# Scan inputs for four states at a time on four 32-row tiles of TensorE

## The chip, the cores and the metric

The kernel runs on one core of one Trainium2 chip. The metric is device microseconds of one launch, the median of several runs. In this text PE is TensorE, DVE is VectorE, ACT is ScalarE, POOL is GpSimd, SP is SyncE (it issues the DMAs).

## The reference, cut to what matters

A four-layer state-space model (Mamba blocks) runs over 16 sequences of 64 context tokens and then 512 tokens, width 256, inner width 512, 16 states; after it comes a cross-attention block with an MLP. All is fp32. What the change touches is the scan input of each layer:

```python
xi = silu(conv(...)); dt = softplus(...)            # [B, S, 512]
dA  = exp(dt[..., None] * A)                        # [B, S, 512, 16]
dBu = dt[..., None] * Bm[:, :, None, :] * xi[..., None]
h = da * h + dbu                                    # a step of the scan over time
y = einsum('bes,bs->be', h, c)                      # sum over the 16 states
```

## The kernel before

**Steps.** Time is always 512 positions. A step is one layer for 512 positions: 8 steps come first for the contexts (two halves, four layers; "the context steps"), then four blocks of 16 steps (four sequences, four layers; "the main steps"), each block followed by the attention. The 512 inner channels are 4 groups (`c`) of 128 partitions, so a step has 4 x 16 = 64 scans of 128 x 512, one for each state and group. They go in 32 units `v` of two states, 8 units to a group.

**One unit.** ACT writes the two decays `dA` (L673, three units ahead, ring of 8). PE writes the two inputs `dBu` into PSUM: `make_input` (L437) multiplies `dtxT` (time on partitions, `dt * xi`) by `diagB`, a diagonal matrix of -B that POOL builds (L1147). Before, the 128 rows of time are two tiles of 64 rows; each tile writes its own bank, and the columns hold (time, state) with two states side by side. Each unit has two banks of four, so the inputs of unit v+1 are made while unit v is scanned: PE waits only for the scans up to unit v-1 (L432). DVE runs the two scans (L912) and reads the PSUM columns at a stride of two. POOL multiplies both by C (L1139). PE sums the states with transposes into one accumulator (`sum_pair`, L454, for unit v-2); ACT takes it out when a group ends (L684).

**The other work of a step** (norm, projections, convolution taps, softplus, gate, residual) belongs to the step before or to the ones after, and is placed by hand in tables: `MAIN_PE`, `MAIN_ACT`, `MAIN_DVE`, `MAIN_POOL` say behind which unit each piece stands on its engine, with the number of steps that it is ahead; `PRE_*` say it for the context steps. A DVE event could stand behind either scan of a unit. PE's pieces share three PSUM banks (`MAIN_BANK`). Each engine goes through its list in order; semaphores tie them. PE pieces: `xi`, `z`, `out` (projections, L479, L484, L517), `xp` (L490), `dt` (L500), `dxT` (L505), `yt` (L510), `bT` (L494), `ms` (L473). DVE events: `tap` (L940), `q` (L946), `less` (L951), `ndt` (L957), `gate` (L962), `res` (L967), `norm` (L922). POOL: `dtx` (L1159), whose result `dxT` turns. SP issues the loads of C, of initial states and of weights (`body` of the last block below).

Of the kernel before, what the change touches and what calls it, by code (L numbers as in the profile page):

```python
# [38 lines left out]
PRE_BANK = {"yt3": 0, "out0": 0, "out1": 1, "dxT1": 0, "dt3": 1, "dxT2": 2, "dxT3": 2, "ms": 0, "xi0": 0, "xi1": 1,  # L39
            "xi2": 2, "xi3": 0, "yt0": 1, "z0": 2, "z1": 0, "z2": 2, "xp": 1, "z3": 0, "bT": 1, "yt1": 0, "dt0": 2,  # L40
            "dt1": 1, "yt2": 0, "dxT0": 0, "dt2": 2}
MAIN_BANK = {"xi0": 0, "xi1": 2, "xi2": 1, "xi3": 0, "dt3": 2, "yt3": 1, "out0": 1, "xp": 2, "dxT3": 0, "bT": 0,
             "dt0": 2, "out1": 1, "yt0": 0, "z0": 0, "dxT0": 2, "z1": 1, "dt1": 2, "yt1": 0, "z2": 1, "z3": 0,
             "dt2": 2, "dxT1": 1, "ms": 0, "yt2": 1, "dxT2": 2}
# [1329 lines left out]
```

## Time and profile before

| what | value |
|---|---|
| median of 3 runs | 9753.2 us (9751.4 to 9761.05) |
| the profiled execution | 9749.7 us, span 9747.6 us |
| PE busy | 8898.7 us, 91% |
| DVE busy | 7469.1 us, 77% |
| POOL busy | 6517.7 us, 67% |
| ACT busy | 5984.7 us, 61% |
| mean granted clock of PE | 0.962 |

Busy time is the union of the instructions of an engine. The mean duration of an instruction is longer than its share of the busy time where several are in flight at once. A matmul in fp32 is two PE instructions, a transpose is one.

### The profile page before, as it was taken

Reading aid. Unit: us, or ns where it says so; the run is one execution under the profiler, and the core shown is the slowest. Engines: PE = TensorE matmul, PEld = TensorE weight load, DVE = VectorE, ACT = ScalarE, POOL = GpSimd, SP = SyncE. Lnnn points to the kernel's source line nnn. Section 1 sums busy time; section 2 is a strip of 40 time slices with the busy share of each in tenths; the row PEclk is TensorE's granted clock in tenths of the full one; section 3 lists DMA queues with packets and bytes.
Section 4 is the critical chain, followed back from the end, with each engine's and each line's share of the span. In section 5 each row is a group of like instructions: output and inputs, shape, how many; then the busy total and the mean of one; then the engine's idle time right before and its main releaser. Section 6 shows DMA issues by size and latency. Waiting matters only on the chain.

```text
span 9747.6 us, 188863 instructions
## 1 busy us (share of the span) xinstructions
PE 8898.7 (91%) x67488; PEld 6199.9 (64%) x67488; DVE 7469.1 (77%) x7810; ACT 5984.7 (61%) x9252; POOL 6517.7 (67%) x3556
## 2 busy tenths in 40 slices
PE   8999799999998799999988799999988799999988
PEld 5666466666664566666654576666654576666654
DVE  5778688888873588888873688888873688888872
ACT  6666576666743566676642566667642666766642
POOL 5878577788761477787751477887751577877750
PEclk9999899999999899999999899999999899999999
DMA  1111111111100111111100111111100111111100
GB/s 56 46 46 41 54 42 39 42 43 55 39 33 6 56 42 39 42 49 48 39 32 7 55 42 39 46 52 42 39 32 8 54 42 39 54 46 40 39 32 9
DMA packets 132793, 390.13 MB, mean 40 GB/s; under 512 B 49520, under 2 KB 77620, under 8 KB 94984
## 3 DMA queue, kind: packets, MB, share of 16 engines
q1 hardware_dynamic: 131848, 377.75, 11.0%
q8 instruction: 566, 9.27, 0.4%
q14 instruction: 379, 3.10, 0.1%
HBM read 364.46 MB, written 13.24 MB: 39 GB/s over the span
## 4 chain that ended last, share of the span: by engine, by line
POOL 48%; issue 38%; PE 3%; POOLq 1%; DVE 1%; ACT 0%; DVEq 0%; ACTq 0%
POOL arena L1139 40%; POOL arena L1147 5%; POOL arena L1159 2%; PE ps L540 1%; POOL arena L1177 1%; PE ps L621 1%; POOLq L1135 1%; DVE arena L1080 0%; DVE arena L1071 0%; ACT arena L824 0%; PE ps L587 0%; PE ps L616 0%; PE ps L517 0%; POOLq L314 0%; DVE arena L1084 0%
## 5 line engine op out<-in xcount | busy, mean ns | idle before, releaser
L1139 POOL TENSOR_TENSOR arena<-arena 128x1024 f32<-128x1024 f32 x2304 | 5441.6, 2366 | 1471.4 <-DVE arena L912 1428.0
L912 DVE TENSOR_TENSOR_SCAN arena<-arena,ps 128x512 f32<-128x512 f32 x4608 | 5606.8, 1259 | 763.1 <-PE ps L437 589.7
L673 ACT ACTIVATE arena<-arena,rate 128x512 f32<-128x512 f32 (+1 forms) x4608 | 3103.8, 713 | 782.7 <-DVE arena L912 771.0
L437 PE MATMUL ps<-arena 64*128 64x128 f32 x36864 | 2711.3, 287 | 345.7 <-DVE arena L912 343.0
L437 PEld LDWEIGHTS ps<-arena 64*128 64x128 f32 x36864 | 2266.8, 189 | 775.4 <-DVE arena L912 481.1
L454 PEld LDWEIGHTS ps<-csts,arena 128*128 128x128 f32 x18432 | 2133.2, 143 | 839.5 <-issue 622.5
L454 PE MATMUL ps<-csts,arena 128*128 128x128 f32 x18432 | 2462.4, 277 | 32.9 <-POOL arena L1139 32.9
L1159 POOL TENSOR_TENSOR arena<-arena 128x512 f32<-128x512 f32 x288 | 365.5, 1269 | 778.5 <-DVE arena L957 778.5
L1147 POOL TENSOR_TENSOR arena<-csts,arena 128x512 f32<-128x512 f32 x576 | 608.5, 1059 | 76.3 <-ACT arena L764 76.3
L788 ACT ACTIVATE arena<-arena,Dall 128x512 f32<-128x512 f32 x288 | 208.3, 723 | 719.3 <-POOL arena L1159 719.3
L517 PE MATMUL ps<-arena 128*128 128x512 f32 x1152 | 630.5, 641 | 7.6 <-DVE arena L962 4.4
L484 PE MATMUL ps<-arena 128*128 128x512 f32 x1152 | 634.7, 642 | 2.7 <-DVE arena L940 2.7
L479 PE MATMUL ps<-arena 128*128 128x512 f32 x1152 | 577.6, 628 | 34.0 <-DVE arena L922 33.4
L540 PE MATMUL ps<-arena 128*128 128x512 f32 (+2 forms) x1152 | 564.4, 646 | 31.7 <-ACT arena L884 16.2
L1177 POOL TENSOR_TENSOR arena<-arena 128x512 f32<-128x512 f32 x128 | 133.2, 1042 | 601.4 <-DVE arena L1074 601.4
L684 ACT ACTIVATE arena<-ps 128x512 f32<-128x512 f32 x288 | 170.8, 593 | 592.5 <-PE ps L454 591.8
L940 DVE SCALAR_TENSOR_TENSOR ps<-arena,ps 128x512 f32<-128x512 f32 x576 | 427.3, 742 | 90.4 <-ACT ps L727 86.8
L540 PEld LDWEIGHTS ps<-arena 128*128 128x128 f32 (+1 forms) x1152 | 240.7, 218 | 372.2 <-issue 350.0
L1106 DVE COPY arena<-ps 128x256 f32<-128x256 f32 x64 | 27.2, 425 | 478.2 <-PE ps L621 478.2
L824 ACT ACTIVATE arena<-ps 128x512 f32<-128x512 f32 (+1 forms) x252 | 137.5, 585 | 387.9 <-PE ps L540 319.5
L951 DVE SCALAR_TENSOR_TENSOR ps<-arena,ps 128x512 f32<-128x512 f32 x288 | 198.0, 687 | 193.5 <-ACT ps L779 192.8
L479 PEld LDWEIGHTS ps<-arena 128*128 128x128 f32 x1152 | 202.9, 195 | 224.7 <-issue 178.3
(102 smaller groups left out, 7640.7 us busy)
## 6 DMA issues: line engine op xcount, KB each, us to landing
arena<-c_rows SPq DMA_DIRECT2D x288, 1024.0 KB, 4.7
arena<-ip_x SPq DMA_DIRECT2D x20, 512.0 KB, 3.6
arena<-ip_z SPq DMA_DIRECT2D x20, 512.0 KB, 3.6
arena<-op_w SPq DMA_DIRECT2D x20, 512.0 KB, 3.9
hT<-xT SPq DMA_DIRECT2D x16, 512.0 KB, 5.2
arena<-w SPq DMA_DIRECT2D x8, 1024.0 KB
out<-arena SPq DMA_DIRECT2D x64, 128.0 KB, 1.7
arena<-xp_w SPq DMA_DIRECT2D x20, 160.0 KB, 2.5
```

Of the source, the lines that this page charges most:

```text
L437: i = nc.tensor.matmul(o, dtxT[rows, c, b, :], diagB[rows, pair, b, :].rearrange("p (i s) -> p i s", s=2), start=True, stop=True)
L454: i = nc.tensor.matmul(acc[:, b * P:(b + 1) * P], hs[:, place(n, v) + s, b * P:(b + 1) * P], eye, start=False, stop=(v + 1) % CU == 0 and ...
L479: i = nc.tensor.matmul(o, ipx[:, k, c * P:(c + 1) * P], xn[:, k, :], start=k == 0, stop=k == KD - 1)
L484: i = nc.tensor.matmul(o, ipz[:, k, c * P:(c + 1) * P], xn[:, k, :], start=k == 0, stop=k == KD - 1)
L517: i = nc.tensor.matmul(o, opw[:, k, c * P:(c + 1) * P], zs[:, par, k, :], start=k == 0, stop=k == KI - 1)
L540: last = nc.tensor.matmul(o, lhs, rhs, start=i == 0, stop=i == len(parts) - 1)
L673: nc.scalar.activation(o, i, ACT.Exp, scale=rate[:, ph.layer(n), g:g + 1]).then_inc(decay.sem, 1)
L912: nc.vector.tensor_tensor_scan(hs[:, place(n, v) + g % 2, :], dA[:, g % RING, :], both[:, g % 2::2], init[:, n % 2, g:g + 1] if ph.main() ...
L940: i = nc.vector.scalar_tensor_tensor(o, w, taps[:, c, k:k + 1], acc_c, ALU.mult, ALU.add)
L1139: nc.gpsimd.tensor_tensor(hs[:, a:a + 2, :], hs[:, a:a + 2, :], Crep[:, 2 * pair:2 * pair + 2, :], ALU.mult).then_inc(prod.sem, 1)
L1147: nc.gpsimd.tensor_tensor(diagB[:, pair, :, :].rearrange("p b (i s) -> p b i s", s=2), minus64.unsqueeze(1).unsqueeze(3).broadcast_to([P, ...
L1159: nc.gpsimd.tensor_tensor(dtx, dt[:, c, :], xs[:, m % 2, c, :], ALU.mult).then_inc(dtx_ready.sem, 1)
```

## The change

Scans are served in sets of four states ("quads"): a set fills all four banks. There are 16 sets in a step instead of 32 pairs. The time rows of `dtxT` are now four tiles of 32 rows, each with a bank of its own, 16 matmuls (32 PE instructions) to a set; the scans read at a stride of four. Set w may be written only when the last scan of set w-1 is done, and it stands at the end of an odd unit on PE, behind that unit's pieces and sum. DVE events now stand only behind both scans of a unit, and the tables place all of them behind odd units, so between the sets. `diagB` is built in four instructions instead of eight a step, `zs` (the z branch) has three buffers instead of two and the z projections are made a step ahead. All tables and bank assignments are new; pieces `xp`, `out`, `xi`, `z`, `ms` are cut less finely. In the context steps one SILU table load and one LOG_EXP load go.

```diff
+Q = 4
+QUADS = G // Q
+CQ = DS // Q
+ZS = 3
...
+MAIN_PE = {2: [("xi3", 1), ("z0", 1)], 4: [("dt3", 0), ("z1", 1)], 6: [("yt3", -1), ("z2", 1)],
+           8: [("xp.0", 1), ("xp.1", 1), ("z3", 1)], 9: [("xp.2", 1), ("xp.3", 1)], 10: [("out0.0", -1), ("out0.1", -1)],
+           11: [("out0.2", -1), ("out0.3", -1)], 12: [("bT", 1), ("dt0", 1)], 13: [("dxT3", 0)],
+           14: [("yt0", 0), ("out1.0", -1)], 15: [("out1.1", -1), ("out1.2", -1)], 16: [("out1.3", -1), ("dt1", 1)],
+           18: [("ms", 2)], 20: [("dxT0", 1)], 22: [("yt1", 0)], 23: [("dt2", 1)], 24: [("dxT1", 1)], 25: [("xi0", 2)],
+           28: [("yt2", 0), ("xi1", 2)], 30: [("dxT2", 1)], 31: [("xi2", 2)]}
+MAIN_DVE = {1: [("tap12", 1), ("tap20", 1)], 3: [("tap21", 1), ("tap22", 1)], 5: [("tap30", 1), ("tap31", 1), ("tap32", 1)],
+            7: [("q3", 0), ("gate3", -1)], 9: [("less3", 0)], 11: [("ndt3", 0)], 13: [("res0", -1)],
+            15: [("q0", 1), ("gate0", 0)], 17: [("less0", 1), ("res1", -1), ("ndt0", 1)], 19: [("q1", 1)],
+            21: [("less1", 1), ("norm0", 2), ("ndt1", 1)], 23: [("norm1", 2), ("gate1", 0)], 25: [("q2", 1)],
+            27: [("less2", 1), ("tap00", 2), ("ndt2", 1)], 29: [("gate2", 0), ("tap01", 2), ("tap02", 2)],
+            31: [("tap10", 2), ("tap11", 2)]}
+MAIN_POOL = {12: [("dtx3", 0)], 18: [("dtx0", 1)], 22: [("dtx1", 1)], 28: [("dtx2", 1)]}
+PRE_PE = {0: [("dxT1", 0)], 2: [("dxT2", 0)], 3: [("yt3", -1)], 4: [("dxT3", 0), ("out0", -1)], 5: [("out1", -1)],
+          8: [("ms", 1)], 12: [("xi0", 1), ("xi1", 1)], 13: [("xi2", 1)], 15: [("xi3", 1)], 16: [("yt0", 0)],
+          18: [("z0", 1), ("z1", 1)], 20: [("z2", 1), ("z3", 1)], 21: [("xp", 1)], 22: [("yt1", 0)], ...
...
-                pe.wait_ge(state.sem, state.at(ph, n, 2 * v - 2))
+                pe.wait_ge(state.sem, state.at(ph, n, Q * w))
                 for b in range(NB):
-                    for h in range(2):
-                        rows = slice(64 * h, 64 * h + 64)
-                        o = input_ps[:, bank + h, :].rearrange("p (i b s) -> p i b s", b=NB, s=2)[:, :, b, :]
+                    for r in range(4):
+                        rows = slice(32 * r, 32 * r + 32)
+                        o = input_ps[:, r, :].rearrange("p (i b s) -> p i b s", b=NB, s=Q)[:, :, b, :]
...
             def body(ph, n):
                 for v in range(UNITS):
-                    to, w = ahead(ph, n, v + 1)
-                    if to is not None:
-                        make_input(ph, to, w)
                     for m, name in events(ph.pe_at, ph, n, v):
                         job(ph, m, name)
                     to, w = ahead(ph, n, v - 2)
                     if to is not None and (scans(ph, n) or n == ph.steps):
                         sum_pair(ph, to, w)
+                    to, w = ahead(ph, n, v + 1)
+                    if to is not None and v % 2:
+                        make_input(ph, to, w // 2)
...
+                if g % Q == 0:
+                    dve.wait_ge(input_ready.sem, input_ready.at(ph, n, g // Q + 1))
...
-                nc.vector.tensor_tensor_scan(hs[:, place(n, v) + g % 2, :], dA[:, g % RING, :], both[:, g % 2::2],
+                nc.vector.tensor_tensor_scan(hs[:, place(n, v) + g % 2, :], dA[:, g % RING, :], quad[:, g % Q::Q],
```

## Rows read from the trace of the kernel before

**Rows 1.** The page: busy time by engine, and the chain that ended last.
```profile
PE 8898.7 (91%) x67488; PEld 6199.9 (64%) x67488; DVE 7469.1 (77%) x7810; ACT 5984.7 (61%) x9252; POOL 6517.7 (67%) x3556
...
POOL 48%; issue 38%; PE 3%; POOLq 1%; DVE 1%; ACT 0%; DVEq 0%; ACTq 0%
```

**Rows 2.** Busy time in two single main steps and six context steps (columns named above them).
```profile
core 0: us, PE busy (x) PEld busy (x) DVE busy (x) ACT busy (x) POOL busy (x), PEclk, DMA share, GB/s
1208.10:1319.00 110.90, 105.24 (x889) 76.47 (x888) 96.93 (x98) 77.09 (x119) 88.04 (x46) 1.00 0.11 42
1319.00:1429.90 110.90, 106.70 (x889) 77.81 (x888) 96.93 (x97) 77.17 (x119) 88.05 (x45) 0.98 0.15 50
...
199.50:907.90 708.40, 658.05 (x5325) 480.44 (x5324) 558.44 (x577) 476.69 (x726) 565.72 (x457) 0.95 0.14 46
```

**Rows 3.** Groups by line, ten main steps (1208.1 to 2316.7 us).
```profile
L912 DVE TENSOR_TENSOR_SCAN arena<-arena,ps 128x512 f32<-128x512 f32 x640 | 784.0, 1266 | 102.2 <-PE ps L437 92.2 <-ACT arena L673 10.1
...
L437 PE MATMUL ps<-arena 64*128 64x128 f32 x5120 | 375.1, 286 | 48.1 <-DVE arena L912 48.0
...
L1139 POOL TENSOR_TENSOR arena<-arena 128x1024 f32<-128x1024 f32 x321 | 758.5, 2367 | 228.7 <-DVE arena L912 227.5
L1147 POOL TENSOR_TENSOR arena<-csts,arena 128x512 f32<-128x512 f32 x80 | 84.8, 1060 | 0.0
L1159 POOL TENSOR_TENSOR arena<-arena 128x512 f32<-128x512 f32 x40 | 50.8, 1270 | 0.0
```

**Rows 4.** Timeline, PE and DVE, where the scans wait for PE.
```profile
2017.09 2.45 DVE L912 TENSOR_TENSOR_SCAN arena<-arena,ps 128x512 f32<-128x512 f32 x2
...
2018.66 1.04 PE L454 MATMUL ps<-csts,arena 128*128 128x128 f32 x8
...
2019.62 1.16 PE L437 MATMUL ps<-arena 64*128 64x128 f32 x16
...
2020.71 1.12 PE L517 MATMUL ps<-arena 128*128 128x512 f32 x2
2020.92 2.45 DVE L912 TENSOR_TENSOR_SCAN arena<-arena,ps 128x512 f32<-128x512 f32 x2 [1.39 <-PE ps L437]
...
2021.68 0.64 PE L505 MATMUL ps<-csts,arena 128*128 128x128 f32 x4
```

**Rows 5.** Timeline where taps stand between scans.
```profile
1985.34 1.16 PE L437 MATMUL ps<-arena 64*128 64x128 f32 x16
...
1986.43 1.98 PE L479 MATMUL ps<-arena 128*128 128x512 f32 x4
...
1988.99 0.73 DVE L940 SCALAR_TENSOR_TENSOR ps<-arena,ps 128x512 f32<-128x512 f32 x1
...
1989.76 0.75 DVE L940 SCALAR_TENSOR_TENSOR arena<-arena,ps 128x512 f32<-128x512 f32 x1
...
1990.42 1.28 DVE L912 TENSOR_TENSOR_SCAN arena<-arena,ps 128x512 f32<-128x512 f32 x1
```

**Rows 6.** Timeline of the four column tiles in the attention: the burst, its first 0.03 us.
```profile
2957.77 1.94 PE L587 MATMUL ps<-arena 128*32 128x512 f32 x8 [5.30 <-ACT arena L824]
...
2957.77 1.08 PE L587 MATMUL ps<-arena 128*32 128x512 f32 x4 [5.30 <-ACT arena L824]
```

**Rows 7.** Busy time and granted clock in short stretches, columns as in rows 2.
```profile
1332.70:1336.10 3.40, 1.41 (x15) 1.17 (x14) 3.36 (x5) 2.38 (x5) 0.85 (x2) 1.00 0.04 3
...
1336.10:1339.50 3.40, 3.40 (x24) 2.94 (x22) 3.40 (x5) 3.37 (x3) 2.23 (x2) 0.50 0.46 154
...
1443.50:1446.90 3.40, 1.41 (x14) 1.17 (x12) 3.36 (x5) 2.38 (x5) 0.85 (x2) 1.00 0.00 0
1446.90:1450.30 3.40, 2.09 (x24) 1.73 (x24) 3.40 (x5) 3.37 (x3) 2.31 (x1) 1.00 0.00 0
```

**Rows 8.** Timeline of PE where the clock is at 0.50.
```profile
1335.88 1.90 PE L437 MATMUL ps<-arena 64*128 64x128 f32 x16 [1.99 <-DVE arena L912]
1337.70 1.96 PE L454 MATMUL ps<-csts,arena 128*128 128x128 f32 x8
```

More of the change, by code:

```diff
@@ L36 @@
 SILU = "silu_and_others"
[L39 to L44, printed above, removed]
@@ L72 @@
-MAIN_PE = {0: [("xi2", 1)], 1: [("xi3", 1)], 2: [("dt3", 0)], 3: [("yt3", -1)], 5: [("out0.0", -1)],
[7 rows of a table removed]
-MAIN_ACT_FIRST = {2: [("yev3", -1)], 10: [("yev0", 0)], 18: [("yev1", 0)], 26: [("yev2", 0)]}
-MAIN_ACT = {0: [("xi1", 1)], 1: [("xi2", 1)], 2: [("xi3", 1)], 3: [("dt3", 0)], 4: [("silu_z", 0), ("silu_x", 1)],
[4 rows of a table removed]
-MAIN_DVE = {(0, 0): [("tap02", 1)], (0, 1): [("tap10", 1)], (1, 0): [("tap11", 1), ("tap12", 1)],
[6 rows of a table removed]
-MAIN_POOL = {7: [("dtx3", 0)], 15: [("dtx0", 1)], 23: [("dtx1", 1)], 28: [("dtx2", 1)]}
+PRE_BANK = {"dt0": 2, "dt1": 0, "dt2": 2, "dt3": 0, "dxT0": 1, "dxT1": 1, "dxT2": 2, "yt3": 1, "out0": 0, "out1": 2,
+            "dxT3": 1, "ms": 1, "xi0": 0, "xi1": 2, "xi2": 1, "xi3": 0, "yt0": 2, "z0": 2, "z1": 1, "z2": 2, "z3": 0,
+            "xp": 1, "yt1": 0, "bT": 1, "yt2": 1}
@@ new lines @@
+MAIN_BANK = {"xi0": 2, "xi1": 1, "xi2": 2, "xi3": 0, "z0": 1, "z1": 1, "z2": 1, "z3": 1, "dt3": 2, "yt3": 0, "xp": 0,
+             "out0": 1, "bT": 0, "dt0": 2, "dxT3": 0, "yt0": 0, "out1": 1, "dt1": 0, "ms": 2, "dxT0": 1, "yt1": 1,
+             "dt2": 0, "dxT1": 1, "yt2": 0, "dxT2": 0}
+PARTS = {"ms": KD, "xi": KD, "z": KD, "xp": KI, "out": KI}
+PRE_PE = {0: [("dxT1", 0)], 2: [("dxT2", 0)], 3: [("yt3", -1)], 4: [("dxT3", 0), ("out0", -1)], 5: [("out1", -1)],
[4 rows of a table added]
+PRE_ACT_FIRST = {2: [("yev3", -1)], 10: [("yev0", 0)], 18: [("yev1", 0)], 26: [("yev2", 0)]}
@@ new lines @@
+PRE_ACT = {0: [("ln3", 0)], 1: [("dxT1", 0), ("skip2", 0)], 3: [("dxT2", 0), ("skip3", 0)], 5: [("dxT3", 0)],
[4 rows of a table added]
+PRE_DVE = {1: [("less3", 0), ("ndt3", 0)], 3: [("gate3", -1)], 5: [("res0", -1)], 7: [("res1", -1)],
[6 rows of a table added]
+PRE_POOL = {0: [("dtx2", 0)], 2: [("dtx3", 0)], 28: [("dtx0", 1)], 30: [("dtx1", 1)]}
+MAIN_PE = {2: [("xi3", 1), ("z0", 1)], 4: [("dt3", 0), ("z1", 1)], 6: [("yt3", -1), ("z2", 1)],
[5 rows of a table added]
+MAIN_ACT_FIRST = {2: [("yev3", -1)], 10: [("yev0", 0)], 18: [("yev1", 0)], 26: [("yev2", 0)]}
+MAIN_ACT = {0: [("xi2", 1)], 3: [("xi3", 1), ("z0", 1)], 5: [("dt3", 0), ("z1", 1)], 6: [("silu_z", 0), ("silu_x", 1)],
[4 rows of a table added]
@@ L198, in program @@
         Crep = view(DS, T)
-        diagB = view(CU, NB, 128)
+        diagB = view(CQ, NB, P)
         dA = view(RING, T)
@@ L204, in program @@
         xs = view(2, KI, T)
-        zs = view(2, KI, T)
+        zs = view(ZS, KI, T)
         xbc = view(2, NB, DS)
@@ L516, in job @@
                     for k in parts:
-                        i = nc.tensor.matmul(o, opw[:, k, c * P:(c + 1) * P], zs[:, par, k, :],
+                        i = nc.tensor.matmul(o, opw[:, k, c * P:(c + 1) * P], zs[:, m % ZS, k, :],
                                              start=k == 0, stop=k == KI - 1)
@@ L729, in event @@
                 elif name[0] == "z":
-                    if m > 1:
-                        await_done(act, ph, m - 2, "out1")
+                    if m >= ZS:
+                        await_done(act, ph, m - ZS, "out1")
                     await_done(act, ph, m, name)
-                    nc.scalar.activation(zs[:, par, c, :], job_bank(ph, name), ACT.Copy).then_inc(read_of(ph, name), 1)
+                    nc.scalar.activation(zs[:, m % ZS, c, :], job_bank(ph, name), ACT.Copy).then_inc(read_of(ph, name), 1)
                 elif name == "silu_z":
-                    nc.scalar.preload_act_table_set(SILU)
-                    await_read_of(act, ph, m, "z2")
-                    await_read_of(act, ph, m, "z3")
-                    nc.scalar.activation(zs[:, par, :, :], zs[:, par, :, :], ACT.Silu).then_inc(silu.sem, 1)
+                    if ph.main():
+                        nc.scalar.preload_act_table_set(SILU)
+                    for k in (3,) if ph.main() else (1, 2, 3):
+                        await_read_of(act, ph, m, f"z{k}")
+                    nc.scalar.activation(zs[:, m % ZS, :, :], zs[:, m % ZS, :, :], ACT.Silu).then_inc(silu.sem, 1)
                     if not ph.main() or m + 1 == ph.steps:
@@ L747, in event @@
                     nc.scalar.activation(xs[:, par, :, :], xs[:, par, :, :], ACT.Silu).then_inc(silu.sem, 1)
-                    nc.scalar.preload_act_table_set(LOG_EXP)
+                    if ph.main():
+                        nc.scalar.preload_act_table_set(LOG_EXP)
                 elif name == "xp":
@@ L961, in event @@
                     await_done(dve, ph, m, f"yt{c}")
-                    nc.vector.tensor_tensor(zs[:, par, c, :], job_bank(ph, f"yt{c}"), zs[:, par, c, :], ALU.mult
+                    nc.vector.tensor_tensor(zs[:, m % ZS, c, :], job_bank(ph, f"yt{c}"), zs[:, m % ZS, c, :], ALU.mult
                                             ).then_inc(read_of(ph, f"yt{c}"), 1)
@@ L974, in body @@
                             scan(ph, n, 2 * v + s)
-                        for m, name in events(ph.dve_at, ph, n, (v, s)):
-                            event(ph, m, name)
+                    for m, name in events(ph.dve_at, ph, n, v):
+                        event(ph, m, name)
             def begin(ph):
@@ L1140, in product, with diag @@
                                         ).then_inc(prod.sem, 1)
-            def diag(ph, m, pair):
-                if pair == 0:
+            def diag(ph, m, quad):
+                if quad == 0:
                     await_read_of(pool, ph, m, "bT")
-                pool.wait_ge(input_ready.sem, input_ready.at(ph, m - 1, UNITS - CU + pair + 1))
-                nc.gpsimd.tensor_tensor(diagB[:, pair, :, :].rearrange("p b (i s) -> p b i s", s=2),
-                                        minus64.unsqueeze(1).unsqueeze(3).broadcast_to([P, NB, 64, 2]),
-                                        xbc[:, m % 2, :, 2 * pair:2 * pair + 2].unsqueeze(2).broadcast_to([P, NB, 64, 2]),
+                pool.wait_ge(input_ready.sem, input_ready.at(ph, m - 1, QUADS - CQ + quad + 1))
+                shape = [P, NB, 32, Q]
+                nc.gpsimd.tensor_tensor(diagB[:, quad, :, :].rearrange("p b (i s) -> p b i s", s=Q),
+                                        minus32.unsqueeze(1).unsqueeze(3).broadcast_to(shape),
+                                        xbc[:, m % 2, :, Q * quad:Q * quad + Q].unsqueeze(2).broadcast_to(shape),
                                         ALU.mult).then_inc(diag_ready.sem, 1)
@@ L1168, in body @@
                         event(ph, m, name)
-                    if v >= UNITS - CU and ph.has(n, 1):
-                        diag(ph, n + 1, v - (UNITS - CU))
+                    if v >= UNITS - CU and v % 2 == 0 and ph.has(n, 1):
+                        diag(ph, n + 1, (v - (UNITS - CU)) // 2)
             def attend(ph):
@@ L1314, in _inputs @@
     p = np.arange(P)
-    cst = np.zeros((P, 321), np.float32)
+    cst = np.zeros((P, 289), np.float32)
     cst[:, 0:128] = p[:, None] == p[None, :]
     cst[:, 128:256] = 1.0 / D
-    cst[:, 256:320] = -1.0 * (p[:, None] % 64 == p[None, :64])
-    cst[DR + DS, 320] = 1.0
+    cst[:, 256:288] = -1.0 * (p[:, None] % 32 == p[None, :32])
+    cst[DR + DS, 288] = 1.0
     cst_attention = np.zeros((P, 424), np.float32)
```

30 lines of the change are left out of this document (12 added, 18 removed), and 51 rows, old and new, of tables (MAIN_ACT, MAIN_DVE, MAIN_PE, PRE_ACT).

## The prediction, made before the changed kernel ran

> **What bounds the kernel now.** I read the page's busy line and chain first. PE is busy for 91% of the span, DVE 77%, and the chain gives POOL 48% and issue 38% [rows 1]. That chain is a poor guide: POOL's products sit idle 227.5 us in ten main steps waiting for scans [rows 3], so POOL follows. Then I cut the span into steps. A main step takes 110.9 us; in it PE is busy 105.2 to 106.7, DVE 96.9, POOL 88.0, ACT 77.1 [rows 2]. There are 64 such steps, so 64 x 110.9 = 7095 us of the 9749.7 of the profiled execution; the 8 context steps are 118.1 each (708.4 / 6, rows 2), 945 us; the rest, some 1710 us, is attention and the ends of the blocks, which the change leaves alone. Third, who waits: the scans wait 92.2 us in ten steps for the inputs (L437), 9.2 a step, and the inputs wait for scans 48.0 [rows 3]. The timeline shows how: transposes, inputs and a projection follow each other on PE without a hole while the scans stand idle 1.39 us [rows 4]. So PE bounds long parts of a step, DVE is 14 us below it.
>
> **What goes.** A pair of inputs holds PE for 2020.71 - 2019.62 = 1.09 us [rows 4], 32 times a step, 34.9 us (the union is 37.5, rows 3). Its 16 instructions last 1.16 us together, and 8 single transposes of the same 128 columns last 1.04 [rows 4], so in the pair two instructions run at a time. A set has 32 instructions. If four run at a time, a set costs what a pair does now: 16 x 1.1 = 17.5 us a step, 17.4 less than before. Four row tiles are in no row. The nearest is the attention's four column tiles: eight instructions in 1.94 us, of which four start within 0.03 us and last to 1.08 [rows 6], so four at a time there. The bounds are 1.1 us a set (four at a time) and 2.0 (two at a time, as the 64-row tiles now); I take 1.1, the value by the column tiles. Four `diagB` instructions of 1.06 [rows 3] go from POOL, 4.2 us a step, as good as nothing, since POOL waits for the scans; so do two table loads in a context step, as ACT has 34 us of slack in a step [rows 2].
>
> The Trainium skill (TensorE: Matmul & The Clock Gate, Part 3 on packing) gives 3.07 times for four row tiles of K=32 at N=512. No run here shows it; by it a set would be near 1.1 us as well, and two at a time unlikely.
>
> **What comes: a wait at each set.** Before, inputs for the next pair were made under a scan. Now PE may start a set only when the fourth scan ends. From the end of a scan to the first input: scans end at 2017.09 + 2.45 = 2019.54, the inputs start at 2019.62, 0.08. From there to the next scan: 2020.92 - 2019.62 = 1.30 [rows 4]. Scans follow each other every 2.45 - 1.27 = 1.18 us [rows 3, 4]. So from the fourth scan's start to the fifth's: 1.27 + 0.08 + 1.30 = 2.65 instead of 1.18, and a set takes 3 x 1.18 + 2.65 = 6.19 us. Sixteen are 99.0 us, with room of 1.47 us for vector work at each boundary. The 32 events of a step cost (96.9 - 78.4) / 32 = 0.58 each [rows 2, 3], dependent taps 0.77 and 0.66 [rows 5]. One or two of them fit; five boundaries have three: behind v=5 three taps (2.2, so 0.7 over), behind 17, 21, 27 and 29 about 1.75 (0.3 over each), together 1.8. DVE's own path is then 100.8 us. A boundary with one event (9, 11, 13, 19, 25) leaves some 0.9 us of DVE empty. The stride of four on the PSUM reads has no row; scans at a stride of two take 1.18; I take 0 and hold 0 to 0.03 us for it, 2 us a step at most.
>
> **Where PE is late for a boundary.** Of 6.19 us the set takes 1.09 and two sums 2 x 0.96 [rows 4], which leaves 3.2 for pieces. Four 512-column instructions take about 1.83 (1.98 with the tail, rows 5), two 0.97, four transposes about 0.5 [rows 4], the start of a group 0.44 more (in sets 1, 5, 9, 13). By the new table, in sets (units 2w, 2w+1):
> - set 1: `xi3` and `z0`, 3.66 + 0.44: 0.9 late;
> - set 4: `xp` 3.66 and `z3` 1.83: 2.3 late;
> - set 5: `out0` 3.66 + 0.44: 0.9 late;
> - set 7: `yt0`, three parts of `out1`, 3.3: 0.1 late;
> - set 6: the pieces fit, but PE waits for POOL. `dtx3` stands behind product 12: 1.18 + 1.27 until unit 12 is scanned, 2.37 for its product, 1.27 for `dtx3` [rows 3], 6.09 us after the set's first scan. Then `dxT3` 0.5, sum 11 0.96, and 1.30: the next scan starts at 8.85, 2.7 late. Before, the same pieces stood two units apart.
> All others need 2.9 or less. Together 6.9, so 107.7 us a main step if PE runs at its full clock, 3.2 less than 110.9. The context steps have the same boundaries; there set 2 (`dxT3`, `out0`, `out1`) and set 10 (`z2`, `z3`, `xp`) are each over 4 us late, set 6 (three `xi`) 2.3, set 9 0.9, and 4 or 5 us of events lie over: 99 + 11.7 + 5 = 115.6, 2.5 less. ACT must make 64 decays and needs 77.1 us in all, POOL 84: neither gets to the path but through `dtx3`. The SP queue issues the same DMAs; `ipz` is loaded later in relation to its first use (20 units ahead still) and `init`, `cinit` and C's rows keep their place, so nothing there. Sum so far: 64 x -3.2 + 8 x -2.5 = -225 us.
>
> **The clock.** The granted clock of PE is at one of two levels, 2.4 GHz (1.00) and 1.2 (0.50). Between 1332.7 and 1336.1 PE was busy 1.41 of 3.4 us, having waited 1.99 us for a scan; in the next 3.4 us the clock was 0.50, though PE was busy throughout. The same stretch one step later, 1443.5, brought no fall [rows 7]. In the main steps this is the one hole, and the fall comes in every second step (1.00 and 0.98, rows 2). At the low clock the inputs last 1.90 instead of 1.16 and eight transposes 1.96 instead of 1.04 [rows 8]. The change makes many such holes: in sets 0, 10 and 13 PE has 0 to 0.5 us of pieces, so it stands 2.7 to 3.2 us of 6.19 idle; sets 6 (the wait for `dtx3`) and 11 have 1.6 to 2.5. A hole of 2 us now brings a fall in half of the cases; so I take 3 falls a step. A fall of 3.4 us takes 1.7 us of PE's work; behind set 0 it lies on set 1, which is late already and pays all of it; elsewhere the boundary pays 0.8 to 0.9 for the slow set, and the sums and pieces doubled use up the slack. The floor is 0 (falls only in slack, as now), the ceiling five falls of 1.7, 8.5 us. I take 3 x 1.7 = 5.0 a step, in a context step 4 (it falls already to 0.95, rows 2): +320 + 32 = +352 us.
>
> The Trainium skill (TensorE: Matmul & The Clock Gate, "HAM oscillation") tells of kernels whose gaps in matmul work bring the low clock back over and over. It speaks against this change; rows 7 show the fall behind such a gap, with the 3.4 us.
>
> **Sum.** 9749.7 - 225 + 352 = 9877; the profiled execution is 3.5 below the median, so 9880 us, 1.3% slower.
>
> **Rivals.**
> - *The clock stays up where it counts.* All steps as above, but the falls hit slack: 0 to 1 us a step. For it: now a fall every second step costs nothing that shows, 110.9 with and without [rows 2]. Against: those steps wait for something else there, and a set at the low clock now is on DVE's path. 9753 - 225 + 40 = 9570 us, faster. It decides from 3.5 us of falls a step: under that the change wins.
> - *Two tiles at a time.* The change doesn't do what it says: 32-row tiles start in twos. Each set is 0.9 longer; 11 boundaries pay all, 5 about 0.6, and PE saves nothing: 13 us a step, so 107.7 + 13 + some 4 of falls = 124.5; 9753 + 64 x 13.6 + 8 x 10 = 10700 us. For it: two at a time is all that row tiles show [rows 4]. Against: rows 6.
> - *The terms cancel*, 3.5 us of falls against 3.2 of gain: 9750, no change.
>
> **How the numbers follow.** Forecast 0.50 (its own range 9770 to 10010: falls of 4 to 7 us), the clock rival 0.30, two at a time 0.13, cancelled 0.07. A run of this kernel can tell 0.2%, 20 us, from no change. Faster 0.31, within it 0.07, slower 0.62. The range of 8 in 10 goes from 9540, which takes in nearly all of the clock rival, to 10150, which takes in the ceiling of the falls with 2 us a step for the stride; two at a time stays outside.
>
> **What would show it.** Right: L437 busy about 18 us a main step; from the fourth scan to the fifth 2.65 us where no more than two events stand; set 6 near 8.9 us and set 4 near 8.5; PEclk 0.93 to 0.95 in the main steps; PE busy near 90 us a step, inputs' wait for scans up. Wrong: a set of inputs at 2 us; PEclk at 0.98 with main steps of 108; scans slower than 1.18 apart; idle DVE released by ACT rather than by L437.

## The result, and the profile after

The changed kernel takes 10052.9 us (median of 4 runs, 10052.2 to 10059.1) against 9752.3 us of the kernel before (4 runs on the same chip): ratio 1.031, interval 1.029 to 1.032. It is slower by 3.1%; I had forecast 1.3%. The profiled execution has a span of 10057.2 us, and the mean granted clock of PE fell from 0.962 to 0.897.

The page of the kernel after, busy time by engine and the chain:
```profile
PE 8118.1 (81%) x67488; PEld 5503.6 (55%) x67488; DVE 7453.2 (74%) x7810; ACT 6004.4 (60%) x9236; POOL 6231.1 (62%) x3268
...
POOL 43%; issue 30%; PE 11%; DVE 3%; ACT 1%; POOLq 1%; DMA 0%; SPq 0%; DVEq 0%; ACTq 0%
```
Against [rows 1], PE has lost 781 us of work and the kernel has become 310 us slower: there is less work on the busiest engine, and more waiting. The same stretches as in [rows 2], and then the last step of a block, which I had not looked at (us, busy time of PE, PEld, DVE, ACT, POOL, granted clock):
```profile
1471.00:1584.90 113.90, 94.55 (x891) 66.56 (x890) 96.56 (x96) 77.70 (x120) 84.16 (x41) 0.93 0.11 41
1584.90:1700.00 115.10, 95.04 (x891) 66.60 (x890) 96.56 (x96) 77.70 (x120) 83.87 (x41) 0.91 0.12 42
...
206.70:930.00 723.30, 585.54 (x5328) 420.58 (x5328) 558.90 (x577) 463.22 (x714) 540.52 (x433) 0.88 0.14 45
2839.40:2947.90 108.50, 75.44 (x789) 62.40 (x787) 81.94 (x73) 49.64 (x69) 75.94 (x33) 0.82 0.03 11
```
The last step of the same block in the kernel before:
```profile
2757.40:2844.50 87.10, 80.64 (x814) 65.60 (x814) 81.52 (x73) 49.63 (x73) 81.61 (x38) 1.00 0.07 26
```
A main step is 113.9 us on average (110.9 before), a context step 723.3 / 6 = 120.6 (118.1). But the last step of a block goes from 87.1 to 108.5, at a clock of 0.82 instead of 1.00. (Here and below, the mean of a main step, of its sets and of its time at the low clock is taken over steps 3 to 13 of all four blocks, from the scans' start times and the granted clock.)

Groups by line of the kernel after, ten main steps, answering to [rows 3]:
```profile
L912 DVE TENSOR_TENSOR_SCAN arena<-arena,ps 128x512 f32<-128x512 f32 x640 | 766.7, 1260 | 172.5 <-PE ps L435 128.2 <-ACT arena L671 43.3
L1139 POOL TENSOR_TENSOR arena<-arena 128x1024 f32<-128x1024 f32 x321 | 756.0, 2362 | 299.9 <-DVE arena L912 299.9
...
L435 PE MATMUL ps<-arena 32*128 32x128 f32 x5120 | 211.7, 308 | 113.7 <-DVE arena L912 113.7
```
The inputs (now L435) fell from 37.5 to 21.2 us a step, as the change promises. The scans wait for them 12.8 us a step (9.2 before) and for the decays 4.3 (1.0 before); the inputs wait for scans 11.4 (4.8). The end of set 5 and set 6 of a main step (counted from 0) on the timeline, where most is lost. The columns are start, duration, engine and line, and in brackets the idle time before and what ended it:
```profile
1627.16 1.04 PE L452 MATMUL ps<-csts,arena 128*128 128x128 f32 x8
...
1628.13 1.18 PE L435 MATMUL ps<-arena 32*128 32x128 f32 x32
...
1629.46 4.79 DVE L912 TENSOR_TENSOR_SCAN arena<-arena,ps 128x512 f32<-128x512 f32 x4 [1.47 <-PE ps L435]
...
1631.99 2.35 POOL L1139 TENSOR_TENSOR arena<-arena 128x1024 f32<-128x1024 f32 x1 [2.15 <-DVE arena L912]
...
1634.30 1.26 POOL L1160 TENSOR_TENSOR arena<-arena 128x512 f32<-128x512 f32 x1
...
1635.62 1.13 PE L503 MATMUL ps<-csts,arena 128*128 128x128 f32 x4 [3.60 <-POOL arena L1160]
1636.54 1.92 PE L452 MATMUL ps<-csts,arena 128*128 128x128 f32 x8
...
1638.39 1.99 PE L435 MATMUL ps<-arena 32*128 32x128 f32 x32
...
1640.61 2.45 DVE L912 TENSOR_TENSOR_SCAN arena<-arena,ps 128x512 f32<-128x512 f32 x2 [5.77 <-PE ps L435]
```
The first set of inputs takes 1.18 us: 32 instructions, where 16 took 1.16 [rows 4], so four run at a time. Then PE stands 3.60 us until POOL has made `dtx3` (L1160), and what follows runs at half speed: `dxT3` 1.13, the sum 1.92, the inputs 1.99 us. Busy time and granted clock of that hole and of the 6.8 us behind it (both are means: between 1633.4 and 1640.1 us the clock is 0.50 throughout, before and after it 1.00):
```profile
1633.00:1635.50 2.50, 0.00 (x0) 0.00 (x0) 1.84 (x3) 2.44 (x5) 2.50 (x2) 0.56 0.00 0
1635.50:1642.30 6.80, 6.68 (x56) 5.70 (x57) 1.70 (x2) 1.90 (x4) 2.38 (x2) 0.66 0.01 2
```
The set takes 11.15 us here from its first scan to the next set's, 10.9 on average. At the end of set 4 the decays are late too, though the prediction saw only PE there:
```profile
1620.24 1.04 PE L452 MATMUL ps<-csts,arena 128*128 128x128 f32 x8
...
1621.21 1.18 PE L435 MATMUL ps<-arena 32*128 32x128 f32 x32
1621.32 0.60 ACT L682 ACTIVATE arena<-ps 128x512 f32<-128x512 f32 x1 [2.08 <-PE ps L452]
1621.81 1.32 ACT L671 ACTIVATE arena<-arena,rate 128x512 f32<-128x512 f32 x2
...
1622.61 3.62 DVE L912 TENSOR_TENSOR_SCAN arena<-arena,ps 128x512 f32<-128x512 f32 x3 [3.22 <-ACT arena L671]
```
ACT takes the accumulator out (L682) only when PE has made the last sum of the group, which stands behind `xp` and `z3`, and the decays stand behind that on ACT.

### The profile page after: what moved, and what is told of

The parts are those of the page before. It is cut to its first block, busy times and chain, and to the rows that moved or that the text cites. A ratio compares the mean times of both kernels' runs of the same rounds, so it can differ in the third digit from the quotient of the medians.

```text
span 10057.2 us, 188207 instructions
## 1 busy us (share of the span) xinstructions
PE 8118.1 (81%) x67488; PEld 5503.6 (55%) x67488; DVE 7453.2 (74%) x7810; ACT 6004.4 (60%) x9236; POOL 6231.1 (62%) x3268
## 4 chain that ended last, share of the span: by engine, by line
POOL 43%; issue 30%; PE 11%; DVE 3%; ACT 1%; POOLq 1%; DMA 0%; SPq 0%; DVEq 0%; ACTq 0%
POOL arena L1139 39%; PE ps L538 6%; POOL arena L1160 2%; PE ps L619 2%; POOL arena L1148 2%; DVE arena L1080 1%; ACT arena L824 1%; DVE arena L1071 1%; PE ps L585 1%; PE ps L515 1%; PE ps L477 0%; PE ps L614 0%; POOLq L1135 0%; DVE arena L1084 0%; PE ps L616 0%
## 5 line engine op out<-in xcount | busy, mean ns | idle before, releaser
L912 DVE TENSOR_TENSOR_SCAN arena<-arena,ps 128x512 f32<-128x512 f32 x4608 | 5490.1, 1254 | 1366.2 <-PE ps L435 945.7
L671 ACT ACTIVATE arena<-arena,rate 128x512 f32<-128x512 f32 (+1 forms) x4608 | 3183.7, 716 | 2032.7 <-DVE arena L912 2025.3
L452 PEld LDWEIGHTS ps<-csts,arena 128*128 128x128 f32 x18432 | 2230.0, 149 | 760.3 <-issue 462.6
L452 PE MATMUL ps<-csts,arena 128*128 128x128 f32 x18432 | 2506.1, 287 | 167.6 <-POOL arena L1139 167.5
L435 PE MATMUL ps<-arena 32*128 32x128 f32 x36864 | 1544.2, 311 | 931.4 <-DVE arena L912 930.9
L435 PEld LDWEIGHTS ps<-arena 32*128 32x128 f32 x36864 | 1305.7, 211 | 1198.8 <-DVE arena L912 1040.9
L1160 POOL TENSOR_TENSOR arena<-arena 128x512 f32<-128x512 f32 x288 | 366.4, 1272 | 803.5 <-DVE arena L957 803.5
L503 PE MATMUL ps<-csts,arena 128*128 128x128 f32 x1152 | 261.3, 363 | 308.5 <-POOL arena L1160 303.3
L940 DVE SCALAR_TENSOR_TENSOR ps<-arena,ps 128x512 f32<-128x512 f32 x576 | 428.4, 744 | 39.1 <-ACT ps L725 33.4
L477 PEld LDWEIGHTS ps<-arena 128*128 128x128 f32 x1152 | 261.2, 250 | 273.1 <-issue 261.8
L503 PEld LDWEIGHTS ps<-csts,arena 128*128 128x128 f32 x1152 | 181.8, 213 | 377.8 <-POOL arena L1160 305.3
L482 PEld LDWEIGHTS ps<-arena 128*128 128x128 f32 x1152 | 211.0, 197 | 310.8 <-issue 239.0
L498 PE MATMUL ps<-arena 33*128 33x512 f32 x576 | 347.2, 686 | 30.0 <-DVE arena L957 30.0
```

The lines of the kernel that those rows point to most:

```text
L435: i = nc.tensor.matmul(o, dtxT[rows, c, b, :], diagB[rows, quad, b, :].rearrange("p (i s) -> p i s", s=Q), start=True, stop=True)
L452: i = nc.tensor.matmul(acc[:, b * P:(b + 1) * P], hs[:, place(n, v) + s, b * P:(b + 1) * P], eye, start=False, stop=(v + 1) % CU == 0 and ...
L477: i = nc.tensor.matmul(o, ipx[:, k, c * P:(c + 1) * P], xn[:, k, :], start=k == 0, stop=k == KD - 1)
L482: i = nc.tensor.matmul(o, ipz[:, k, c * P:(c + 1) * P], xn[:, k, :], start=k == 0, stop=k == KD - 1)
L503: i = nc.tensor.matmul(o[:, b * P:(b + 1) * P], dtx[:, b::NB], eye, start=b == 0, stop=b == NB - 1, is_transpose=True)
L671: nc.scalar.activation(o, i, ACT.Exp, scale=rate[:, ph.layer(n), g:g + 1]).then_inc(decay.sem, 1)
```

## Experiments

Each is timed against the kernel before, on the same chip as it. In the code, "the changed kernel" is the one of the diff above.

**1. `dtx3` one unit earlier.** The hole in set 6 comes from POOL; the product in front of `dtx3` is now behind it.
```diff
-MAIN_POOL = {12: [("dtx3", 0)], ...
+MAIN_POOL = {11: [("dtx3", 0)], ...
```


> The changed kernel with one entry moved: POOL's dtx3 behind unit 11 instead of behind unit 12 (main steps only). Theory (the loss is made at the boundaries between the sets, and one of its parts is that PE waits for POOL in front of dxT3 in set 6): set 6 falls from 10.9 us to 6.5, the clock fall behind that hole goes too, a main step from 113.9 to about 109.6, the whole to about 9790 us, faster than the changed kernel by 2 to 3%. Rival (set 6 only shows first what sets 7 and 8 would lose anyway, since PE has the same pieces to do): sets 7 and 8 grow by what set 6 gives, a main step stays above 112.5 and the whole above 9970 us.

Measured: 9825.7 us, ratio 1.007 (1.006 to 1.009), 227 less than the changed kernel; I had expected some 9790, and the rival, that sets 7 and 8 take the gain back, is refuted. A main step is 110.3 us, 3.6 less; set 6 takes 6.9 instead of 10.9, so it gives 4.0, and the other sets lose 0.3 of it again (set 7 takes 6.56 instead of 6.18). On PE there now:
```profile
1978.01 1.17 PE L435 MATMUL ps<-arena 32*128 32x128 f32 x32 [0.46 <-DVE arena L912]
1979.34 0.75 PE L503 MATMUL ps<-csts,arena 128*128 128x128 f32 x4 [0.16 <-POOL arena L1160]
...
1984.19 1.17 PE L435 MATMUL ps<-arena 32*128 32x128 f32 x32 [1.41 <-DVE arena L912]
```
The wait for `dtx3` is down to 0.16 us, and the inputs behind it (1984.19) run at full speed. One entry in a table carries 2.3 of the 3.1%. The time at the low clock goes from 17.8 us a step to 14.4, and it differs by block of the one execution: in the first and third block it is 17.8 and a main step 111.2 us, in the second and fourth 11.6 and 109.5. The program is the same in all four, so the difference of 1.8 us is a price of the clock.

**2. PE kept busy in three holes.** Ten useless matmuls a step (128 x 256, into a bank whose owner comes next, nothing reads them) behind the sums of units 1, 21 and 27; the kernel computes all that the reference asks.
```diff
+FILL = {1: [("xi3", 1, 3)], 21: [("yt1", 0, 4)], 27: [("xi1", 2, 3)]}
...
+            def fill(ph, m, name, times):
+                pe.wait_ge(read_of(ph, name), bank_free(ph, m, name))
+                for _ in range(times):
+                    nc.tensor.matmul(job_bank(ph, name)[:, 0:256], ones_x, csts[:, 0:256], start=True, stop=True)
...
```


> The changed kernel with useless matmuls in three holes of PE of a main step: 3, 4 and 3 matmuls of 128x256, their results overwritten unread, behind the sums of units 1, 21 and 27, ahead of the wait for the next boundary. Theory (the falls of PE's clock cost time on DVE's path): the time at the low clock goes from 18.6 us a main step to about 9 (the fall behind the wait for dxT3 stays), a main step from 113.9 to about 111.5, the whole to about 9900 us. Rival (the falls hit slack, the time is made by turnaround and late pieces alone): the granted clock rises as much, but a main step stays within 0.7 us of 113.9, the whole at 10020 to 10080 us.

Measured: 9997.3 us, ratio 1.025 (1.024 to 1.027). A main step is 112.6 us, low clock 11.2 us of it instead of 17.8. Set 0 went from 6.95 to 6.25 and set 1 from 8.22 to 6.85: 2.07 us from one filler. But set 10 grew from 6.55 to 7.81, because there the filler itself waits for its bank, with the inputs behind it:
```profile
1883.74 1.99 PE L524 MATMUL ps<-csts 128*128 128x256 f32 x8 [1.52 <-ACT arena L794]
1885.67 1.17 PE L436 MATMUL ps<-arena 32*128 32x128 f32 x32
```
So the falls cost time, which the rival denied, and the filler that I put into the wrong bank gave more than half of it back. The result lies between what theory and rival gave.

**3. Two tiles at a time.** The changed kernel with 64-row tiles again, in sets of four. The waits and the tables are the same. With the tiles two smaller things go back as well: `diagB` is built in eight instructions, and the scans read at a stride of two.
```diff
-                for b in range(NB):
-                    for r in range(4):
-                        rows = slice(32 * r, 32 * r + 32)
...
+                for pair in range(2):
+                    for b in range(NB):
+                        for h in range(2):
+                            rows = slice(64 * h, 64 * h + 64)
...
```


> The changed kernel, its tables and its sets of four states, but each set is made by two pairs as in the kernel before: 64-row tiles, 16 matmuls, diagB in eight instructions. So the tile width alone is undone. Theory (four tiles run at a time and save 0.9 us at every boundary): a set of inputs lasts 2.05 us instead of 1.18, the fourth to the fifth scan 3.5 us instead of 2.65, a main step 122 to 126 us, the whole 10650 to 10850 us. Rival (PE has slack in most sets, and its holes and clock falls go as it gets busier): a main step 115 to 118, the whole under 10300 us.

Measured: 10839.7 us, ratio 1.112 (1.110 to 1.114), a main step 124.0 us. The timeline:
```profile
1991.93 2.06 PE L436 MATMUL ps<-arena 64*128 64x128 f32 x32 [0.76 <-DVE arena L914]
```
A set costs 2.06 us instead of 1.18, and from the fourth scan to the fifth it takes 3.50 instead of 2.64. This is the rival "two tiles at a time" as a kernel (I had put it at 124.5 a step and 10700 us). The packing is worth 10.1 us a step in the changed kernel; what else the change brings, the single set of banks above all and the new tables with it, takes all of that and 3.0 us more. No run has the new tables with two sets of banks, so the two are not told apart.

**4. The single buffer without the packing.** The kernel before, with one change: the pair of inputs is made at the end of a unit, when both scans are done.
```diff
-                pe.wait_ge(state.sem, state.at(ph, n, 2 * v - 2))
+                pe.wait_ge(state.sem, state.at(ph, n, 2 * v))
...
-                    to, w = ahead(ph, n, v + 1)
-                    if to is not None:
-                        make_input(ph, to, w)
...
+                    to, w = ahead(ph, n, v + 1)
+                    if to is not None:
+                        make_input(ph, to, w)
```


> The kernel before, with its tables, pairs and 64-row tiles, but the inputs of pair v+1 are made at the end of unit v on PE and wait for the scans of unit v too: one buffer in use instead of two, nothing else changed. Theory (the second buffer hides the turnaround of 2.65 against 1.18 us from scan to scan): a unit takes 1.18 + 2.65 us at least, 32 of them 122.6, with the events behind first scans on top a main step takes 125 to 130 us; the last step of a block, 85.9 us from its first to its last scan before, 120 or more; the whole 10700 to 11000 us. Rival (PE is the bound, so its inputs are late with two buffers as well): a main step under 115 us, the whole under 10050 us.

Measured: 11979.4 us, ratio 1.229 (1.226 to 1.231), main step 140.3 us. The direction is as expected, the size is not: I had 125 to 130 a step and 10700 to 11000 us. The last step of a block goes from at most 85.9 us, first scan to last, to 124.0 to 127.4 (expected: 120 or more). The timeline, scans on DVE and inputs on PE:
```profile
2290.74 2.45 DVE L912 TENSOR_TENSOR_SCAN arena<-arena,ps 128x512 f32<-128x512 f32 x2 [1.35 <-PE ps L437]
2294.54 2.45 DVE L912 TENSOR_TENSOR_SCAN arena<-arena,ps 128x512 f32<-128x512 f32 x2 [1.35 <-PE ps L437]
```
```profile
2293.24 1.16 PE L437 MATMUL ps<-arena 64*128 64x128 f32 x16 [0.28 <-DVE arena L912]
2294.34 1.13 PE L484 MATMUL ps<-arena 128*128 128x512 f32 x2
2295.39 1.12 PE L500 MATMUL ps<-arena 33*128 33x512 f32 x2
2296.44 1.09 PE L454 MATMUL ps<-csts,arena 128*128 128x128 f32 x8
2297.47 1.16 PE L437 MATMUL ps<-arena 64*128 64x128 f32 x16
```
The boundary costs what it costs in the changed kernel (scan to scan at least 2.61 us), but there are 32 of them, and between two boundaries only the 2.45 us of two scans cover PE's pieces: in the main step from 2212.7 to 2352.7 us the scans wait 41.0 us for inputs. My estimate had counted the boundaries and not the pieces that no longer fit. With the tables of the kernel before, a single set of banks costs 29.4 us a step in pairs; in sets of four, packed and with tables made for it, it costs 3.0.

**5. PE's pieces spread.** Experiment 1, and pieces moved from full sets to empty ones.
```diff
-MAIN_PE = {2: [("xi3", 1), ("z0", 1)], ...
+MAIN_PE = {0: [("xi3", 1)], 2: [("z0", 1)], ...
-           11: [("out0.2", -1), ("out0.3", -1)], 12: [("bT", 1), ("dt0", 1)], 13: [("dxT3", 0)],
-           14: [("yt0", 0), ("out1.0", -1)], 15: [("out1.1", -1), ("out1.2", -1)], 16: [("out1.3", -1), ("dt1", 1)],
+           11: [("out0.2", -1)], 12: [("out0.3", -1), ("bT", 1), ("dt0", 1)], 13: [("dxT3", 0)],
+           14: [("yt0", 0), ("out1.0", -1)], 15: [("out1.1", -1)], 16: [("out1.2", -1), ("out1.3", -1), ("dt1", 1)],
```


> The changed kernel with dtx3 behind unit 11 as in the first experiment, and three of PE's main-step entries moved to sets with room: xi3 from unit 2 to unit 0, the last part of out0 from unit 11 to 12, the third part of out1 from 15 to 16. Theory (pieces that don't fit into the room of a set are paid one for one, and the hole of set 0 brings a clock fall that set 1 pays): set 1 falls from 8.3 us to 6.3 to 6.6, set 0 from 7.1 to 6.2, the time at the low clock by 3 to 5 us a step, a main step from 110.4 to about 107.5, the whole to about 9660 us, faster than both kernels. Rival (PE's work is the same, so it is paid wherever it stands): a main step stays above 109.7, the whole above 9790 us.

Measured: 9560.7 us, ratio 0.980 (0.979 to 0.982): 2.0% faster than the kernel before, where I had expected some 9660. A main step is 105.8 us, low clock 10.0. Twelve steps by line:
```profile
L912 DVE TENSOR_TENSOR_SCAN arena<-arena,ps 128x512 f32<-128x512 f32 x764 | 915.4, 1261 | 108.0 <-ACT arena L671 61.6 <-PE ps L435 43.4
```
Scans wait for inputs 43.4 / 12 = 3.6 us a step, where the changed kernel had 12.8. Against experiment 1, set 0 went from 7.06 to 6.25, set 1 from 8.34 to 6.18, set 5 from 6.82 to 6.18, set 7 from 6.56 to 6.18, and set 2 from 6.93 to 7.86; why set 2 grew no run tells. `xi3` in unit 0 does two things: it leaves set 1, and it fills set 0's hole. The 0.8 us of set 0, which itself got more to do, is what the filler of experiment 2 gave there too, so the fall is gone with the hole.

**6. Spread and filled.** Experiment 5 with eight useless matmuls in the holes of sets 10, 11 and 13; two of the three groups now stand right ahead of the owner of their bank.
```diff
+FILL_FIRST = {20: [("dxT0", 1, 3)], 22: [("yt1", 0, 2)]}
+FILL = {27: [("xi1", 2, 3)]}
```


> The kernel of e6_spread with useless matmuls of 128x256 in holes again, where their bank is free early: 3 in front of dxT0 (unit 20), 2 in front of yt1 (unit 22), 3 behind the sum of unit 27; their results are overwritten unread. Theory (clock falls cost 0.3 to 1 us each on DVE's path in the light sets): the time at the low clock falls by 6 to 9 us a step against e6_spread, sets 10 to 14 get shorter by 1.0 to 2.0 us together, a main step is about 106, the whole 9580 to 9620 us. Rival (in light sets the falls hit slack only): granted clock up, a main step within 0.4 us of e6_spread.

Measured: 9494.7 us, ratio 0.974 (0.972 to 0.976). I had expected 9580 to 9620 from an experiment 5 at 9660; against experiment 5 as measured it is 66 us less, where 40 to 80 were expected. One main step, and the last step of a block:
```profile
1760.54:1865.67 105.13, 92.01 (x905) 64.77 (x904) 96.51 (x96) 77.16 (x120) 84.03 (x41) 0.98 0.15 53
2700.80:2799.90 99.10, 69.44 (x793) 56.95 (x791) 80.67 (x72) 49.56 (x69) 74.65 (x33) 0.91 0.03 12
```
The low clock falls from 10.0 to 1.1 us a step, and a step from 105.8 to 104.3; the last step of a block, in which only the two matmuls of unit 22 stand, from 104.8 to 99.2. By the time that the falls took from PE one would have hoped for more: 8.9 us less at half speed saved 1.4. Sets 10 to 14 gave 0.8 of it (expected: 1.0 to 2.0), and set 2, where nothing was changed, as much again; the other sets lose 0.2. That the falls behind sets 10 to 13 hit slack is the reading that fits; it is not shown by itself.

**7. Filled in set 6 alone.** The changed kernel, `dtx3` as late as it was, three useless matmuls ahead of `dxT3`: the wait stays, the fall goes.
```diff
+FILL_FIRST = {13: [("dxT3", 0, 3)]}
```


> The changed kernel with three useless matmuls of 128x256 in front of dxT3 (unit 13) and nothing else, so that PE works while dtx3 is awaited; the wait itself stays. Theory (set 6 is 10.9 us long by two causes: 2.7 us of waiting for dtx3, and the clock fall behind it, at which dxT3, the sum and the set's inputs run at half speed): set 6 falls from 10.9 us to 8.8 to 9.0, a main step from 113.9 to about 112, the whole to about 9930 us. Rival (the clock has no part, the wait is all): set 6 at 10.5 us or more, the whole above 10020 us.

Measured: 9835.4 us, ratio 1.009 (1.008 to 1.011), a main step 109.9 us. The timeline of PE in set 6 (L525 is the filler, L505 and L1175 are `dxT3` and `dtx3`, L437 the inputs):
```profile
1842.06 1.56 PE L525 MATMUL ps<-csts 128*128 128x256 f32 x6 [0.81 <-ACT arena L779]
1844.86 0.75 PE L505 MATMUL ps<-csts,arena 128*128 128x128 f32 x4 [1.24 <-POOL arena L1175]
1845.45 1.04 PE L454 MATMUL ps<-csts,arena 128*128 128x128 f32 x8
1846.42 1.17 PE L437 MATMUL ps<-arena 32*128 32x128 f32 x32
```
Nothing computed is moved or removed; PE works in the hole, and the set goes from 10.88 to 9.12 us with the inputs at 1.17 instead of 1.99. The wait for POOL is still there: 1.24 us behind the useless matmuls. My prediction for this set without a fall was 8.85. So the 4.0 us that experiment 1 took from it divide into 2.2 of waiting for POOL and 1.8 of clock. The whole kernel did better than expected (112 a step, 9930 us): sets 0, 1, 9 and 11, where nothing was changed, got shorter by 0.44, 0.92, 0.50 and 0.50 us, and the low clock went from 17.8 to 8.1 us a step. Why falls at other places went too, no run of mine tells.

**8. The same for the context steps.** Experiment 6 with `dtx0` one unit earlier there.
```diff
-PRE_POOL = {..., 28: [("dtx0", 1)], ...
+PRE_POOL = {..., 27: [("dtx0", 1)], ...
```


> The kernel of e7_spread_fill with dtx0 behind unit 27 instead of 28 in the context steps, where set 14 lasts 11.1 us. Theory (the same fault as dtx3 in the main steps: dxT0 stands one unit behind its dtx0): set 14 of the context steps falls to 6.7 to 7.2 us, seven of eight steps have it, so 28 us and with the clock fall behind it some 35 us less: about 9460 us. Rival (it moves to set 15 or to the next step): within 10 us of e7_spread_fill.

Measured: 9485.8 us, ratio 0.973 (0.972 to 0.974), which its interval doesn't tell from experiment 6; I had expected 9460, and the rival, within 10 us of experiment 6, is what came. The long set 14 of a context step went from 11.1 to 10.2 us and not below 7.2. PE there:
```profile
430.54 1.09 PE L454 MATMUL ps<-csts,arena 128*128 128x128 f32 x8
435.13 1.13 PE L505 MATMUL ps<-csts,arena 128*128 128x128 f32 x4 [3.49 <-DVE arena L977]
```
The wait now ends with L977. That is `gate2`, an event of DVE behind unit 29: `gate2` reads `yt2` from the PSUM bank that `dxT0` is to write, so `dxT0` can't start before it. POOL's `dtx0` was done by 433.1 us and was not the last. A wait has been taken away, and the next one, 0.9 us below it, is in its place.

## Why the prediction was right in direction and wrong in size

**What goes: right.** Four tiles of 32 rows run four at a time: 1.18 us a set, against 2.06 in two at a time (experiment 3). I had 1.1. L437 was to be busy 18 us a main step; it is 21.2 (now L435), as a part of the sets runs at the low clock. The prediction's estimate by the Trainium skill (TensorE: Matmul & The Clock Gate, Part 3), that 3.07 times would be near 1.1 us as well, is too low: eight single transposes hold PE for 0.96 us [rows 4], so 32 single instructions would take 3.84, and 3.84 / 3.07 = 1.25, an estimate. Counted from the same 3.84, the measured 1.18 is 3.3 times.

**What comes: right.** From the fourth scan to the fifth 2.64 us at the least (sets 3 and 7), forecast 2.65; reading PSUM at a stride of four costs nothing (scans follow each other every 1.18 us, as at a stride of two).

**Where PE is late: right where no fall comes in.** Measured against forecast by set, in us: set 2 6.93 (6.9), set 3 6.17 (6.19), set 4 8.64 (8.5), set 5 6.82 (7.1), set 8 6.49 (6.5), set 10 6.55 (6.5). Above their forecast lie set 0 with 6.95 (6.19) and set 1 with 8.22 (7.1), which experiment 2 brings to 6.25 and 6.85 with the clock held up, and sets 9 and 11 to 14, by 0.4 to 0.5 each. The working found the places; experiments 1 and 5 emptied them and the time went with them. In the context steps, sets 2, 10, 6 and 9 are long by 4.1, 3.4, 2.2 and 0.9 us, where the forecast had over 4, over 4, 2.3 and 0.9; set 14, 11.1 us, it did not have. In set 4 the scan was released by ACT's decays, held by the same pile of pieces. I had given ACT no part ("neither gets to the path but through `dtx3`"), but decays end 4.3 us of waits a step. In experiment 6 they are the larger wait, 4.4 us against 2.9 for inputs.

**Set 6: found, under-priced.** Forecast 8.85, measured 10.88; experiment 7 gives 9.12 with the clock held up. I priced the wait and the falls in separate sums, and here the hole that POOL makes brings the fall onto the very chain that POOL delays.

**The clock: the size right, by two errors.** I took three falls of 3.4 us at 1.7 us each, 5.0 a step. There are four falls in a step, many of them longer, and 17.8 us at the low clock instead of 10.2; the clock of a main step is 0.91 to 0.93, where I had 0.93 to 0.95. The trace of the changed kernel has its own price for them: of the 44 main steps, all of the same program, ten have 13.7 us at the low clock and take 112.6 us on average, fifteen have 17.1 and take 113.9, nineteen have 20.5 and take 114.7. That is 0.3 us for a us of low clock, and 5.3 us a step, an estimate that draws this line down to no low clock at all. The experiments lie around it: by experiment 7 9.6 us less gave 4.0, by experiment 6 8.9 less gave 1.4, by experiment 2 6.6 less gave 1.3, the loss at set 10 included. So a us of low clock costs 0.15 to 0.4 us, less than the half of it that PE loses, and there is more of it than I took; that the product comes near 5.0 is luck. In the kernel before, 21 main steps without a fall and 21 with one of 3.4 us both take 110.9: there the fall did hit slack, as the rival said. For the changed kernel the rival that the clock is harmless is refuted by these steps and by experiments 2, 6 and 7. The rival of two tiles is refuted by the 1.18 us.

The Trainium skill (TensorE: Matmul & The Clock Gate, "HAM oscillation") was the warning that I weighed, and the traces agree: the clock is 0.93 and 0.91 in steps where it was 1.00 and 0.98.

**The term that failed most: "64 x -3.2".** The prediction says "there are 64 such steps, so 64 x 110.9 = 7095" (it is 7098). There are only 60 of them; the other four are the last of their block and took some 87 us. No work of a next step stands beside the scans there, so nothing covers the turnaround: by the prediction's own set of 6.19 us, 15 x 6.19 + 3 x 1.18 = 96.4 us from the start of the first scan to that of the last, where the kernel before had 85.9. I gave them the gain of an ordinary step, which they could not have. The groups by line in the last step, of the kernel after:
```profile
L912 DVE TENSOR_TENSOR_SCAN arena<-arena,ps 128x512 f32<-128x512 f32 x64 | 76.7, 1261 | 28.0 <-PE ps L435 28.0
```
and of the kernel before:
```profile
L912 DVE TENSOR_TENSOR_SCAN arena<-arena,ps 128x512 f32<-128x512 f32 x64 | 76.8, 1263 | 5.2 <-PE ps L437 5.2
```
It measures 107.2 us from first scan to last, 21.3 more. Of these 10.5 are turnaround, and 5.0 are set 6, which takes 11.24 us here with the same wait for `dtx3`. PE stands idle 33 of the 108.5 us, and the clock is 0.82. Experiment 4 shows the turnaround's part by itself: with nothing but the single set of banks the last step goes from 85.9 to 124 and more. In experiments 5 and 6 the step takes 104.8 and 99.2 in the first block.

**The balance.** Of +309.6 us between the profiled executions, the four last steps are 86 (84.4 to 85.9 us before, 106.7 to 107.2 after), the other 60 main steps 60 x 3.1 = 188, and the context phase 36 (its last scan starts at 1034.3 instead of 998.1 us). The forecast had 4 x 1.8 = 7, 60 x 1.8 = 108 and 12, together +127. So 183 us are missing in it: 79 in the last steps, 80 in the ordinary main steps, where set 6 alone is 2.0 us over its forecast, and 24 in the context phase. Half of these 24 are the last context step (from 90.2 to 104.3 us), which has the same gap, and a quarter the first (107.0 to 115.0).

**Open.** Which holes bring a fall: equal sets fall in some steps and not in others, and experiment 7 took falls away at a distance. And no run gives the kernel before new tables of its own, so it is not shown that the packing is needed for the 2.6% that experiment 6 gains.

## What to carry to other kernels

Trading a double buffer for work saved turns hidden time into a turnaround at each refill. Price it in every phase, and first in those where nothing else stands beside it: the last steps of the blocks paid seven times what an ordinary step did (21.3 and 3.1 us). Packing freed PE, but PE then waited, and a wait on TensorE was paid twice where the clock fell behind it on the chain that was late already (set 6: 2.2 us of wait, 1.8 of clock). Look for the one late producer, whose table entry was worth 2.3% here. With `dtx3` a unit earlier, three pieces moved and eight useless matmuls a step, the packed kernel is 2.6% faster than the kernel before; the 0.1% more with the context entry is within the noise. To price a clock that comes and goes, compare steps of the same program inside one trace before building fillers.

## What the runs showed of the hardware

- 16 matmuls in fp32 of 32 rows x 128 columns on four row tiles (32 instructions) end in 1.18 us, on two tiles of 64 rows in 2.06. The Trainium skill (TensorE: Matmul & The Clock Gate, Part 3) has 3.07 times for four tiles; here four tiles run at 1.75 times the rate of two (2.06 / 1.18), and no run here has a single tile to compare.
- Useless matmuls hold the clock up: 1.1 us a step at the low clock with eight of them against 10.0 without, for 3.8 us of PE's time (1.40 for three, 0.96 for two).
- A us at the low clock costs this kernel 0.3 us: main steps with 13.7, 17.1 and 20.5 us of it take 112.6, 113.9 and 114.7 in the changed kernel. In the kernel before a fall of 3.4 us in a main step costs nothing (110.9 with and without).
- With one set of PSUM banks, a refill by PE between DVE's scans makes it 2.64 us from scan to scan instead of 1.18. Of the 1.46 us more, the matmuls are 1.18 and the two hand-overs the rest.
- The scan reads fp32 from PSUM at a stride of four as fast as at two: 4.79 us for four, 2.45 for two.
